# Graph layers on one core: summing casts, ELU inside the accumulator banks, maxima scaled in their pass, and a new order

## What is computed

```python
def gat(x, adj, W, a):                       # layer 0, one head
    h = x @ W
    e = leaky_relu((h @ a1)[:, :, None] + (h @ a2)[:, None, :], 0.2)
    return elu(softmax(where(adj > 0, e, NEG)) @ h)
def transformer(x, adj, ...):                # layer 1, 8 heads of 32
    t = softmax(where(mask, q @ k.T / sqrt(32), NEG)) @ v
    x = layernorm(x + t) * g1 + b1
    return layernorm(x + relu(x @ w1 + b1f) @ w2 + b2f) * g2 + b2
def multi_head_gat(x, adj, W, a): ...        # layer 2: as layer 0, 4 heads of 64, elu
def dot_gat(x, adj, W1, W2, W3):             # layer 3, one head
    e = leaky_relu((x @ W1) @ (x @ W2).T, 0.2)
    return relu(softmax(where(adj > 0, e, NEG)) @ (x @ W3))
x = layernorm(x + gat(x));  x = layernorm(x + transformer(x))
x = layernorm(x + multi_head_gat(x));  x = layernorm(x + dot_gat(x))
```

## Time and profile before

| | us |
|---|---|
| median of 3 runs | 3153.42 |
| lowest, highest | 3149.73, 3153.46 |
| span of the profiled execution, first to last instruction | 3151.5 |
| PE busy | 2825.1 (90%) |
| ACT busy | 2725.2 (86%) |
| DVE busy | 2718.3 (86%) |
| POOL busy | 2484.0 (79%) |

### The profile page before, as it was taken

One profiled execution on the slowest core, in us unless ns is written; L12 is line 12 of the kernel. 1 busy time (PEld: TensorE's weight loads), 2 busy tenths in 40 slices (PEclk: granted clock), 3 DMA queues, 4 the chain that ended last, 5 costly groups with the idle time before them and its releaser, 6 DMA issues. The chain is left out here.

```text
span 3151.5 us, 69440 instructions
## 1 busy us (share of the span) xinstructions
PE 2825.1 (90%) x22576; PEld 1522.9 (48%) x22576; DVE 2718.3 (86%) x7426; ACT 2725.2 (86%) x5847; POOL 2484.0 (79%) x2517
## 2 busy tenths in 40 slices
PE   5898999889999999999999999999999998999864
PEld 4443445445545544544545454554554554445443
DVE  6878788889898989989898998989899898998774
ACT  6668888989899988989998898998889998888884
POOL 6467688777888878788787878878788887867884
PEclk9999999999999999999999999999999999999977
DMA  7335555656656656565656665565665666655454
GB/s 173 79 77 107 123 112 111 132 111 132 128 107 133 128 123 130 122 123 119 136 123 133 125 118 119 124 134 125 131 127 109 131 127 126 129 115 110 99 114 87
DMA packets 1215802, 378.89 MB, mean 120 GB/s; under 512 B 1157712, under 2 KB 1194320, under 8 KB 1215440
## 3 DMA queue, kind: packets, MB, share of 16 engines
q1 hardware_dynamic: 1213616, 373.46, 57.4%
q10 hardware_dynamic: 1824, 0.99, 0.2%
HBM read 21.43 MB, written 16.78 MB: 12 GB/s over the span
## 5 line engine op out<-in xcount | busy, mean ns | idle before, releaser
L883 POOL TENSOR_TENSOR split_r<-prob_r,split_r 128x512 f16<-128x512 f32 x768 | 930.6, 1222 | 251.9 <-DVE split_r L1354 251.9
L1592 PE MATMUL bank_ps<-val_r,trans_r 128*128 128x64 f16 (+1 forms) x9216 | 640.1, 222 | 77.4 <-DMA trans_r<-split_r 76.7
L1354 DVE CAST split_r<-prob_r 128x512 f16<-128x512 f32 x768 | 600.4, 788 | 111.4 <-ACT prob_r L1104 100.8
L1316 DVE CUSTOM_DVE_ANT_0 unused<-bank_ps,neg_mask 128x512 bf16<-128x512 f32 x1024 | 651.1, 683 | 36.8 <-PE bank_ps L1526 34.8
L1592 PEld LDWEIGHTS bank_ps<-val_r,trans_r 128*128 128x128 f16 x9216 | 528.2, 99 | 307.1 <-issue 136.5
L1126 ACT ACTIVATE prob_r<-bank_ps 128x512 f32<-128x512 f32 x1024 | 568.3, 597 | 50.9 <-PE bank_ps L1544 47.2
L1104 ACT ACTIVATE prob_r<-masked_r,low_r 128x512 f32<-128x512 f32 x768 | 553.4, 723 | 58.3 <-DVE low_r L1301 52.9
L1552 PE MATMUL bank_ps<-prob_r,value_ones 128*64 128x512 f32 (+1 forms) x2048 | 557.6, 611 | 3.1 <-ACT prob_r L1126 0.5
L1301 DVE CUSTOM_DVE_ANT_0 masked_r<-bank_ps,neg_mask 128x512 f32<-128x512 f32 x768 | 510.1, 679 | 52.0 <-ACT bank_ps L1092 35.2
L1543 PE MATMUL bank_ps<-stack 98*128 98x512 f16 x1024 | 395.4, 386 | 37.8 <-DVE low L1316 19.8
L1544 PE MATMUL bank_ps<-neg_mask_t,identb 128*128 128x512 bf16 x1024 | 392.0, 383 | 0.0
(11 more groups left out here) (147 smaller groups left out, 4734.1 us busy)
## 6 DMA issues: line engine op xcount, KB each, us to landing
stack<-qk SPq DMA_DIRECT2D x384, 128.0 KB, 2.4
xcur<-in_x_dram SPq DMA_DIRECT2D x32, 512.0 KB, 4.1
out_dram<-z SPq DMA_DIRECT2D x32, 512.0 KB, 3.6
trans_r<-split_r SPq DMA_TRANSPOSE x768, 2.8
xt_r<-split_r SPq DMA_TRANSPOSE x320, 2.8
stack<-low_rows SPq DMA_DIRECT2D x128, 4.0 KB
qk<-in_adj_dram SPq DMA_DIRECT2D x1, 1024.0 KB, 7.8
z<-in_L_gnn_W_dram SPq DMA_DIRECT2D x4, 256.0 KB, 12.4
```

Source lines behind the costliest of these rows:

```text
L883: nc.gpsimd.tensor_tensor(split_r[:, j, 1, :], prob_r[:, i, :], split_r[:, j, 0, :], ALU.subtract).then_inc(lo_done.sem, 1)
L1316: nc.vector.tensor_tensor_reduce(out=unused[:, nth % 2, :], in0=bank_ps[entry("bank", "sq", g, t, b, h)][:], in1=neg_mask[:, b, :], scale= ...
L1354: nc.vector.tensor_copy(split_r[:, entry("split", *unit), 0, :], prob_r[:, entry("prob", *unit), :]).then_inc(hi_dve.sem, 1)
L1592: ins = nc.tensor.matmul(bank[:, at:at + width], trans_r[:, i, pp, jb, :], val(g, layer)[:, vp, jb, cols], start=(n == 0), stop=(n == len( ...
```

## The change

What it does, part by part:

- **Row sums move.** `ex` loses `accum_out`. `hi_v` is no longer a cast (`tensor_copy`) but a `tensor_scalar` (times 1, with an adding accumulator) that writes the f16 part and the row sum. `hid_hi` becomes the same form, its sum going to an unused column (`spare`), with a wait on the one before the last.
- **ELU stays in the accumulator bank.** Layer 0: the exponential is written back into the bank, and `em` reads bank and "a0"; `z` "b0" is gone. Layer 2: `dv` divides in place in the bank, `el` reads the bank, `em` writes max(x,0)+residual into the bank, `es` reads "b2" and the bank and writes "a2". The bank is closed by `em` (layer 0) or `es` (layer 2), where `fo` or `dv` closed it.
- **Maxima scaled in their pass.** `mx` multiplies by a prepared column `low_factor` where it multiplied by -1, and the first of the three instructions of `mh` goes.
- **Spread** waits, before it writes its buffer, for the last reader of it.
- **The plan**: costs are set anew for most kinds (`ex` 0.72 to 0.55, `em` 1.0 and 0.75 to 0.62, `es` 1.15 to 0.62, `lo` 1.22 to 1.13, landing of a transposing DMA 2.7 to 1.6), and the whole table `LATER` is another. Instruction counts on PE, POOL and SP are the same.

The core of the diff:

```diff
-    LATER = {"add_0": 28, "add_1": 13, "add_3": 110, "ap_0": 49, "ap_1": -4, "ap_2": 4, "ap_3": 30, "ap_ffn": -75, "ap_out": 41,
...
+    LATER = {"add_0": 40, "add_1": -12, "add_3": 71, "ap_0": 41, "ap_1": -22, "ap_2": 4, "ap_3": 30, "ap_ffn": 135, "ap_out": 41,
...
-                    task(("xd", *key), 1.25, [("x_lo", *key)], opens=[("xt", (g, phase))], closes=[entry], lands=2.7)
+                    task(("xd", *key), 1.25, [("x_lo", *key)], opens=[("xt", (g, phase))], closes=[entry], lands=1.6)
...
-            task(("ex", *key), 0.72, [("mk", *key)], opens=[("prob", key)], closes=[("masked", key)])
-            task(("hi_v", *key), 0.64, [("ex", *key)], opens=[("split", key)])
-            task(("lo", *key), 1.22, [("hi_v", *key)], closes=[("prob", key)])
+            task(("ex", *key), 0.55, [("mk", *key)], opens=[("prob", key)], closes=[("masked", key)])
+            task(("hi_v", *key), 0.63, [("ex", *key)], opens=[("split", key)])
+            task(("lo", *key), 1.13, [("hi_v", *key)], closes=[("prob", key)])
...
-                 opens=[("trans", key), ("bank", ("acc", g, layer, b // 2))], closes=[("split", key)], lands=2.7)
-            task(("pv", *key), {0: 1.42, 2: 0.38, 3: 1.42}[layer], [("tr", *key)] + value,
+                 opens=[("trans", key), ("bank", ("acc", g, layer, b // 2))], closes=[("split", key)], lands=1.6)
+            task(("pv", *key), {0: 1.34, 2: 0.37, 3: 1.34}[layer], [("tr", *key)] + value,
...
-                    task(("em", g, layer, p), 1.0, [("fo", g, layer, p)], closes=[("z", (g, "b0"))])
-                    task(("add", g, layer, p), 1.27, [("em", g, layer, p)])
+                    task(("em", g, layer, p), 0.62, [("fo", g, layer, p)], closes=[entry])
+                    task(("add", g, layer, p), 1.25, [("em", g, layer, p)])
                 elif layer == 2:
                     task(("el", g, p), 0.53, [("dv", g, layer, p)], opens=[("z", (g, "b2"))])
-                    task(("em", g, layer, p), 0.75, [("el", g, p)])
-                    task(("es", g, p), 1.15, [("em", g, layer, p)], closes=[("z", (g, "b2"))])
+                    task(("em", g, layer, p), 0.62, [("el", g, p)])
+                    task(("es", g, p), 0.62, [("em", g, layer, p)], opens=[("z", (g, "a2"))], closes=[("z", (g, "b2")), entry])
                 else:
...
-            return scaled.at(*key) if key[1] in (0, 3) else divided.at(*key)
+            if key[1] == 0:
+                return elu_max.at(*key)
+            return scaled.at(*key) if key[1] == 3 else elu_sum.at(key[0], key[2])
...
+                    was = prior("spread", g, layer, h)
+                    if was is not None:
+                        act.wait_ge(*leaky_done.last((*was, b) for b in range(NB)))
...
-                    col = COLUMN[layer] + h
                     nc.scalar.activation(prob_r[:, entry("prob", *unit), :], masked_r[:, i, :], ACT.Exp,
-                                         bias=low_r[:, i:i + 1], scale=-1.0,
-                                         accum_out=rowsum[s][:, b, col:col + 1]).then_inc(probs_done.sem, 1)
+                                         bias=low_r[:, i:i + 1], scale=-1.0).then_inc(probs_done.sem, 1)
                 elif kind == "q_hi":
...
                         if layer == 0:
-                            ins = nc.scalar.activation(z(g, "b0")[:, b, :], acc, ACT.Exp, scale=by)
+                            ins = nc.scalar.activation(acc, acc, ACT.Exp, scale=by)
...
-                    nc.scalar.activation(z(g, "b2")[:, pair(p), :], z(g, "a2")[:, pair(p), :], ACT.Exp).then_inc(elu_exp.sem, 1)
+                    nc.scalar.activation(flat(z(g, "b2")[:, pair(p), :]), bank_ps[entry("bank", "acc", g, 2, p)][:],
+                                         ACT.Exp).then_inc(elu_exp.sem, 1)
...
+            after(nc.vector.tensor_scalar(low_factor[:], some_col[:], -LOW_SCALE, None, ALU.mult))
...
-                    nc.vector.tensor_copy(proj(g, "f")[:, n, 0, :], flat(z(g, "a1")[:, pair(n), :])).then_inc(hidden_hi.sem, 1)
+                    nth = hidden_hi.at(g, n)[1]
+                    if nth > 2:
+                        dve.wait_ge(hidden_hi.sem, nth - 2)
+                    nc.vector.tensor_scalar(proj(g, "f")[:, n, 0, :], flat(z(g, "a1")[:, pair(n), :]), 1.0, None, ALU.mult, ALU.add,
+                                            accum_out=spare[:, nth % 2:nth % 2 + 1]).then_inc(hidden_hi.sem, 1)
...
-                                                   in1=neg_mask[:, b, :], scale=-1.0, scalar=BIG, op0=ALU.add, op1=ALU.min,
+                                                   in1=neg_mask[:, b, :], scale=low_factor[:, b:b + 1], scalar=BIG, op0=ALU.add, op1=ALU.min,
...
-                    nc.vector.scalar_tensor_tensor(out=low[s][:, t], in0=low[s][:, t], scalar=LOW_SCALE,
-                                                   in1=some_col[:].unsqueeze(2).broadcast_to([P, NB, QUAD]),
-                                                   op0=ALU.mult, op1=ALU.mult).then_inc(low_chain, 1)
-                    low_links += 1
-                    dve.wait_ge(low_chain, low_links)
...
-                    nc.vector.tensor_copy(split_r[:, entry("split", *unit), 0, :],
-                                          prob_r[:, entry("prob", *unit), :]).then_inc(hi_dve.sem, 1)
+                    layer, h, b = key
+                    col = COLUMN[layer] + h
+                    nc.vector.tensor_scalar(split_r[:, entry("split", *unit), 0, :], prob_r[:, entry("prob", *unit), :], 1.0, None,
+                                            ALU.mult, ALU.add,
+                                            accum_out=rowsum[s][:, b, col:col + 1]).then_inc(hi_dve.sem, 1)
...
-                    was = prior("z", g, "a2")
-                    if was is not None:
-                        dve.wait_ge(*z_free(was))
+                    shares = bank_ps[entry("bank", "acc", g, layer, p)][:].rearrange("p (b h d) -> p b h d", b=2, h=heads)
                     nc.vector.tensor_tensor(
-                        z(g, "a2")[:, pair(p), :].rearrange("p b (h d) -> p b h d", h=heads),
-                        bank_ps[entry("bank", "acc", g, layer, p)][:].rearrange("p (b h d) -> p b h d", b=2, h=heads),
+                        shares, shares,
                         rinv[s][:, pair(p), cols].unsqueeze(3).broadcast_to([P, 2, heads, C // heads]),
                         ALU.mult).then_inc(divided.sem, 1)
...
+                    bank = bank_ps[entry("bank", "acc", g, layer, p)][:]
                     if layer == 0:
                         dve.wait_ge(*scaled.at(g, 0, p))
-                        first, edge, op, other = z(g, "b0"), 1.0, ALU.min, z(g, "a0")
+                        total = flat(z(g, "a0")[:, pair(p), :])
+                        ins = nc.vector.scalar_tensor_tensor(out=total, in0=bank, scalar=1.0, in1=total, op0=ALU.min, op1=ALU.add)
                     else:
                         dve.wait_ge(*elu_exp.at(g, p))
-                        first, edge, op, other = z(g, "a2"), 0.0, ALU.max, xcur[s]
-                    nc.vector.scalar_tensor_tensor(out=z(g, f"a{layer}")[:, pair(p), :], in0=first[:, pair(p), :], scalar=edge,
-                                                   in1=other[:, pair(p), :], op0=op, op1=ALU.add).then_inc(elu_max.sem, 1)
+                        ins = nc.vector.scalar_tensor_tensor(out=bank, in0=bank, scalar=0.0, in1=flat(xcur[s][:, pair(p), :]),
+                                                             op0=ALU.max, op1=ALU.add)
+                    ins.then_inc(elu_max.sem, 1)
                 elif kind == "es":
...
-                    nc.vector.scalar_tensor_tensor(out=z(g, "a2")[:, pair(p), :], in0=z(g, "b2")[:, pair(p), :], scalar=1.0,
-                                                   in1=z(g, "a2")[:, pair(p), :], op0=ALU.min, op1=ALU.add).then_inc(elu_sum.sem, 1)
+                    was = prior("z", g, "a2")
+                    if was is not None:
+                        dve.wait_ge(*z_free(was))
+                    nc.vector.scalar_tensor_tensor(out=flat(z(g, "a2")[:, pair(p), :]), in0=flat(z(g, "b2")[:, pair(p), :]), scalar=1.0,
+                                                   in1=bank_ps[entry("bank", "acc", g, 2, p)][:],
+                                                   op0=ALU.min, op1=ALU.add).then_inc(elu_sum.sem, 1)
```

65 lines of the change are left out of this document (32 added, 33 removed), and 26 rows, old and new, of the table LATER.

## The result

| | before | after |
|---|---|---|
| median, lowest, highest, us | 3153.46, 3149.73, 3155.16 | 3143.29, 3134.41, 3151.3 |
| ratio to before, 95% interval | 1 | 0.9967 [0.9954, 0.998] |
| span of the profiled execution | 3151.5 | 3140.9 |

What follows compares the result with a forecast made beforehand. No engine alone was the bound; PE, DVE and ACT delay each other in turn. DVE -171, ACT -70 and POOL -47 to -105 us would widen PE's lead, cutting its idle time by 131 us: 3022 us, range 2935 to 3115.

Steps and rivals of the forecast that it cites:

- The summing cast at 683: VectorE's 768 unit casts, 788 ns on average, would take 683 in the new accumulating form: -81 us.
- ELU -58: VectorE's `em` and `es`, 188.8 us in three groups of 64, would come near 683 ns each: -58 us.
- `hid_hi` -12: VectorE's 64 `hid_hi` instructions would go from 866 to 683 ns in the accumulating form: -12 us.
- `lo` at its median, -47: GpSimd's 768 `lo` instructions would fall from their mean of 1222 ns to their median of 1161: -47 us.
- ScalarE's read: The accumulator read after `ex` on ScalarE, which fills 57 us alone, would go.
- The rival by the tier rule: VectorE's casts lose a fast mode, +244 us on DVE, giving 3241 us; next to no chance, counted within slower's 0.09.
- the held bank: Slower rival: accumulator bank held through the ELU, some 3.8 us longer 64 times, giving 3205 us; slower in all 0.09.
- the rival "nothing": No gain, 3150 us: the cast's length is the form's price and the new plan gives back ACT's saving; chance 0.05.
- the scale by a column instead of a constant in 1024 maxima: VectorE's layer-1 maxima: the column scale was taken to cost nothing, with a bound of 31 us.
- The first instruction of `mh`: -20.: VectorE's split of the layer-1 maxima loses its first instruction: -20 us.
- a transposing one lands 2.8 us after issue in the median: Transposing DMAs would match the new plan's 2.85 us, where 3.95 kept 1.1 in hand; costed at nothing net.
- If the idle time falls as the lead grows: PE's lead over DVE and ACT grows 2.6 times, so its idle falls from 6.6 to 2.5 us a graph: -131 us.

Runs made afterwards that it cites:

- e7: e3 with the cast of before for `hi_v` and the row sum on ScalarE's exponential again: 3159.6 us.
- e2: The changed kernel with the layer-1 maxima scaled by a constant instead of a column, the factor for nodes without neighbours left out: 3075.96 us.
- e3: The changed kernel with the edits of e1 and e2 together: 3076.52 us.
- e8: The changed kernel with its two new small tiles (`spare`, `low_factor`) allocated last: 3116.69 us.
- e9: e3 with the small tiles allocated last: 3053.43 us.
- e12: e2 with the small tiles allocated last, both f16 parts of the maxima computed: 3053.27 us.
- e11: The kernel before with an added tile of 64 bytes a partition ahead of the small ones, no loop instruction changed: 3159.18 us.
- e4: The changed kernel without the 1024 matmuls that add the mask in layer 1: 3126.12 us.
- e14: e9 without the 1024 matmuls that add the mask in layer 1: 3029.3 us.
- e13: e9 with an accumulator on `ex` again, its sum going to an unused column: 3098.92 us.
- e1: The changed kernel with the two small `mh` instructions as accumulating `tensor_scalar`, the second f16 part written as zero: 3093.41 us.

## Why the prediction was wrong

**Right.** The summing cast at 683: 677, with lengths from 628 to 687 where they had been 365 to 1587, and its accumulator read beside other work, all on this view (duration ns min/median/max):

```profile
L1359 DVE TENSOR_SCALAR_CACHE_REDUCE split_r<-prob_r x768: 628/681/687, 45.5 to 3119.7; 128x512 f16<-128x512 f32 x192
...
L885 POOL TENSOR_TENSOR split_r<-prob_r,split_r x768: 1142/1159/1184, 46.2 to 3120.6; 128x512 f16<-128x512 f32 x192
```

-81 was -90 measured. ELU -58: 188.8 to 130.9, -58, and line 1386, which writes a bank, takes 682 as those that don't. `hid_hi` -12: -12. `lo` at its median, -47: -53, with more than forecast from GpSimd's other work. ScalarE's read: 57 us gone. The rival by the tier rule fell as argued, and so did the held bank: none of PE's or ScalarE's waits names lines 1383, 1386 or 1395. The time came out beside the rival "nothing" (3150), which had 0.05, but not by its reason: the casts did lose their waits, and casts and read together were worth 83 us (e7).

**Wrong, in the order of their cost.**

1. *"the scale by a column instead of a constant in 1024 maxima is taken at nothing"*. It is 60 ns each, 63 us; the bound of +31 was half of it. The reason given, that each already streams 512 elements, doesn't cover it; whether the 60 ns grow with the length no run shows, since all have 512 elements. As the trace of before has no custom instruction with a column there, the bound had to come from a row and was set by feeling (a twentieth).
2. *"The first instruction of `mh`: -20."* The rest of `mh` went from 18.0 + 17.2 to 36.5 + 40.6 us, so it was +22. The prediction had the mechanism in hand ("the operations that stretch are those with two SBUF streams") and used it only for what the change removed. Two such instructions stayed, on the one way by which a graph's layer 1 reaches PE, and in the new order they fell on GpSimd's pair once a graph. Steps 1 and 2 together are 67 us (e2, e3).
3. *"a transposing one lands 2.8 us after issue in the median ... I cost it at nothing net"*. It landed after 3.3, by the place of a tile that two others had pushed on: 23 to 27 us (e8, e9, e12). The list of "would show it wrong" had PE's waits for the DMA, and they grew from 25.7 to 33.5. With the old plan's 1.1 us in hand the same shift costs 7 (e11).
4. *"If the idle time falls as the lead grows"*, 6.6 to 2.5 us a graph. In e12 steps 1 to 3 are mended (`mh` by its place alone) and the engines are where the sum had them: DVE 79.3 us a graph (79.4 forecast), ACT 82.5 (82.4), POOL 72.9 (74.5 to 76.3). PE is busy 85.8, the pace is 90.5 instead of 89.5 and PE idles 4.7 instead of 2.5. That last 1.0 x 32 is the 31 us between 3053 and 3022. The rule gave three quarters of the gain once the work was really gone, but that is luck in part, since its reason doesn't hold: PE isn't the engine that the others run up against at the pace of 93 (e4), and only for about a fifth at 90.8 (e14).
5. ScalarE's `ex` stayed at 727 instead of 695: -15 for -21, small.

90 us of the missing 121 are steps 1 to 3, 31 are step 4. What remains open is what holds the pace at 90.5 us when every engine has less work than that. The runs give only a rate for each: of busy time taken from ScalarE some 0.7 comes out as time (e13), from VectorE 0.3 for the maxima (e1 to e3) and nearly all for `mh` (e1), from PE 0.1 to 0.2 (17 and 24 us of some 145).

## What to carry to other kernels

When a change removes a conflict, look for the instructions of the same kind that stay, however short: 16 elements a partition waited for a whole instruction of another engine, and their place was worth 50 us. Look also at what new small tiles do to the addresses of the large ones behind them, since that lengthened the transposing DMAs without a word in the diff. And before a busy share is taken for a floor, take work away from that engine and see whether the pace moves; here 4.5 us a graph off the busiest one moved it by 0.2 us, and by 1.0 once the other losses were mended. Compare such a run with the very kernel that it was made from.

## What the runs showed of the hardware

- A custom VectorE instruction over 512 elements takes 743 ns with a scale from a column and 683 with a constant (e2); from start to start 0.68 us (1030.15 to 1030.83 above) and 0.61.
- A VectorE cast or difference of 128x16 takes 0.16 to 0.18 us alone and 1.07 to 1.11 us each time that it falls on GpSimd's pair in the steady part of after; as an accumulating form it takes 159 and 170 ns on average and never over 176 (e1).
- Transposing DMAs whose source begins 64 bytes past a multiple of 256 land in 3.3 us in the median, at the multiple in 2.8, and load the queue by a tenth more (e8, e11); a destination 96 bytes past one costs nothing (`xt_r`, 2.8 in e8).
- ScalarE's accumulator read is 197 to 210 ns on average in the profile (before, e7, e13) and adds 65 us of busy time in 768, 85 ns each (e13).
